# Edge preparation merged into the head attention, edge chunks fetched inside the counting stage

## What is computed

```python
def reference(x, src, dst, ...):
    # layer 1: attention among the 8 heads of each node, then a sum over edges
    Q, K, V = (x @ Wq), (x @ Wk), (x @ Wv)                 # each as [N, 8 heads, 32]
    score = softmax(einsum('nhd,ngd->nhg', Q, K) / sqrt(32), axis=-1)
    x1 = einsum('nhg,ngd->nhd', score, V).reshape(N, 256)
    attn_out = segment_sum(x1[dst] * x1[src], dst, N)      # = x1 * (adjacency counts @ x1)
    ...                                                    # O, norm, FFN, norm, GRU, norm
    # layer 2: h = x @ W, weights exp(-leaky_relu(s[src] + t[dst])), a normalised sum over edges
    return layernorm(x + relu(weighted_sum / row_sum))
```

## Time and profile before

| | |
|---|---|
| median of 3 runs | 2529.97 us (2529.07 to 2530.01) |
| profiled execution: its own time | 2528.87 us |
| profiled execution: its span in the trace | 2527.2 us |
| PE busy | 2398.2 us (95% of the span) |
| DVE busy | 1908.9 us (76%) |
| ACT busy | 1309.4 us (52%) |
| POOL busy | 575.0 us (23%) |
| granted TensorE clock, mean | 0.982 |
| preparation | until the first load of the attention at 62.02 us |
| head attention | until the counting's first instruction at 374.48 us |
| counting | until about 1092 us |
| update, then weighing | the rest |

### The profile page before, as it was taken

How to read it: one execution, slowest core, us unless ns; L and a number is a source line. 1 busy time by engine, 2 the same in 40 slices (tenths; PEclk the granted TensorE clock), 3 DMA queues, 4 the chain that set the end, 5 groups by cost and what they waited for, 6 DMA issues and landing times.

```text
span 2527.2 us, 47159 instructions
## 1 busy us (share of the span) xinstructions
PE 2398.2 (95%) x16169; PEld 1994.7 (79%) x16169; DVE 1908.9 (76%) x3148; ACT 1309.4 (52%) x2239; POOL 575.0 (23%) x628
## 2 busy tenths in 40 slices
PE   3899979999999999979999999899999999999995
PEld 2577757877777777756666666699999999999995
DVE  5788866666666666637777776799989898989895
ACT  3233328888888888844444444555343334333432
POOL 4699970000000000024444443000101010101010
PEclk9999998999999999989999999899999999999998
DMA  2111102223223223260214210356464645464552
GB/s 81 54 46 46 46 25 109 110 119 128 110 115 133 110 110 137 110 207 30 68 65 128 74 44 30 90 127 122 93 124 92 123 90 123 97 114 90 121 104 54
DMA packets 406003, 240.04 MB, mean 95 GB/s; under 512 B 326288, under 2 KB 397584, under 8 KB 399568
## 3 DMA queue, kind: packets, MB, share of 16 engines
q1 hardware_dynamic: 397536, 228.12, 32.9%
q10 hardware_dynamic: 7056, 6.43, 0.7%
q0 software_dynamic: 1248, 3.41, 0.5%
HBM read 48.38 MB, written 110.84 MB: 63 GB/s over the span
## 4 chain that ended last, share of the span: by engine, by line
PE 47%; issue 33%; POOL 2%; SPq 1%; DMA 1%; ACT 1%; DVE 0%; POOLq 0%; ACTq 0%; DVEq 0%
PE b_pagg L1500 22%; PE u_hf L632 10%; PE u_mo L616 7%; PE b_pcounts L1511 6%; POOL d_rstd L1848 2%; PE u_tp L605 2%; PE u_tp L676 0%; DMA u_agg<-agg 0%; DMA agg<-b_sums 0%; ACT b_counts L1539 0%; ACT b_counts L1540 0%; SPq L557 0%; SPq L166 0%; SPq L564 0%; SPq L151 0%
## 5 line engine op out<-in xcount | busy, mean ns | idle before, releaser
L1870 PE MATMUL d_acc<-d_rows_high,d_weights_high 128*128 128x258 f32 x2401 | 679.4, 283 | 7.6 <-DVE d_weights_low L1742 5.4
L1871 PE MATMUL d_acc<-d_rows_low,d_weights_high 128*128 128x258 f32 x2401 | 678.2, 282 | 0.0
L1872 PE MATMUL d_acc<-d_rows_high,d_weights_low 128*128 128x258 f32 x2401 | 677.7, 282 | 0.0
L1500 PE MATMUL b_pagg<-x_parts,b_counts 128*128 128x512 f32 x2401 | 608.5, 402 | 0.0
L1819 ACT CAST d_weights_high<-d_weights 128x896 fp32r<-128x896 f32 x343 | 323.5, 944 | 485.7 <-PE d_acc L1872 292.7
L1500 PEld LDWEIGHTS b_pagg<-x_parts,b_counts 128*128 128x128 f32 x2401 | 437.6, 189 | 92.3
L1870 PEld LDWEIGHTS d_acc<-d_rows_high,d_weights_high 128*128 128x128 f32 x2401 | 454.7, 189 | 8.1 <-issue 8.1
L1871 PEld LDWEIGHTS d_acc<-d_rows_low,d_weights_high 128*128 128x128 f32 x2401 | 454.8, 189 | 0.3 <-issue 0.3
L1872 PEld LDWEIGHTS d_acc<-d_rows_high,d_weights_low 128*128 128x128 f32 x2401 | 454.7, 189 | 0.0
L1742 DVE TENSOR_TENSOR d_weights_low<-d_weights,d_weights_high 128x896 fp32r<-128x896 f32 x343 | 373.5, 1089 | 52.9 <-ACT d_weights_high L1819 51.3
L1176 DVE TENSOR_TENSOR b_lo_hot<-b_nodes,b_ends 128x1024 bf16<-128x1024 f16 x392 | 269.9, 688 | 179.6 <-PE b_pcounts L1511 179.2
(11 more groups left out here) (162 smaller groups left out, 2793.8 us busy)
## 6 DMA issues: line engine op xcount, KB each, us to landing
edge_counts<-b_counts SPq DMA_DIRECT2D x49, 1568.0 KB, 5.2
node_table<-u_table SPq DMA_DIRECT2D x7, 903.0 KB, 4.9
qx<-in_x SPq DMA_DIRECT2D x49, 128.0 KB, 2.0
x_table<-x_tile ACTq DMA_DIRECT2D x49, 128.0 KB, 1.7
agg<-b_sums SPq DMA_DIRECT2D x49, 128.0 KB, 4.2
u_x<-x_table SPq DMA_DIRECT2D x7, 896.0 KB, 5.3
u_agg<-agg SPq DMA_DIRECT2D x7, 896.0 KB, 7.4
u_nodes<-in_x SPq DMA_DIRECT2D x7, 896.0 KB, 5.1
```

Of the source, the lines that this page charges most:

```text
L1500: last = nc.tensor.matmul(pagg[:, o, :], ca[:, o, hi, :], x1_parts[:, hi].rearrange("p m d -> p (m d)"), start=(hi == 0), stop=(hi == TILE ...
L1870: nc.tensor.matmul(acc[:, r, 0:HT], a, high[:, t, :], start=(t == 0), stop=False)
L1871: nc.tensor.matmul(acc[:, r, 0:HT], a, low[:, t, :], start=False, stop=False)
L1872: return nc.tensor.matmul(acc[:, r, 0:HT], b, high[:, t, :], start=False, stop=(t == TILES - 1))
```

## The change

One part merges the first two stages. `prepare_edges` is gone; its line search (`find_lines`) now consists of small functions that the attention's own engine programs call at certain steps, so one barrier and one clearing fall away. SP loads `e_dst` ahead of the first tile and the weights, and `e_dst_next` behind the fourth tile. DVE runs the one-hot comparisons ahead of its first step; PE runs the 202 counting matmuls ahead of its step 3; DVE makes the index in its step 1, between the products and their sums; POOL then issues one gather.

A second part moves the chunks. Only chunk 0 is fetched and split in the merged stage (behind DVE's last step), the other 25 in the counting stage: every second step POOL copies one column of the index and issues a gather, DVE splits the ends in six operations behind its batches 3 to 7, SP stores the result to HBM (`edges_found`) and loads it back with a transposing DMA into a buffer for two steps. PE's transposes, ACT's share of the splitting and the big `edge_ends` are gone. The test of the edges compares neighbouring line numbers now (two small matmuls) and stands behind the last step.

A third part swaps two places on ACT: the keys of tile T-1 are copied ahead of the exponential of T-2, not behind it.

The diff, cut to its core:

```diff
-def attention_rows(nc, kit, c, w, x, x1_out, parts):
+def attention_rows(nc, kit, c, w, x, x1_out, dst, pairs, found, chunk, early, parts_after):
...
             @block.sync
...
+                    if isinstance(T, int) and T == QUAD - 1:
+                        lines["load_next"](sp)
+
+                lines["load_dst"](sp)
                 tile_steps(sp, step, 0)
+                lines["first_ends"](sp)
...
             @block.tensor
             def _(pe):
                 def step(T, u):
+                    if isinstance(T, int) and T == 3:
+                        lines["count_lines"](pe)
+                        lines["next_lines"](pe)
...
                 tile_steps(pe, step, 6)
+                lines["sum_bad"](pe)
...
             @block.scalar
...
                         nc.scalar.copy(xT[:, u % 2, :], tpv[:, u % 2, 0:D]).then_inc(xT_ready, 1)
+                    t, q = T - 1, (u - 1) % QUAD
+                    if is_tile(t):
+                        act.wait_ge(qkv_in_psum, T)
+
+                        free(act, products, t, 2)
+                        nc.scalar.copy(keys[:, q % 2, :], pqk[:, q % 2, D:2 * D]).then_inc(k_ready, 1)
                     if is_tile(T - 2):
                         act.wait_ge(shifted, T - 1)
                         q = (u - 2) % QUAD
                         nc.scalar.activation(sc[:, q], sc[:, q], ACT.Exp, scale=SCORE_SCALE).then_inc(exped, 1)
                     t, q = T - 1, (u - 1) % QUAD
                     if is_tile(t):
-                        act.wait_ge(qkv_in_psum, T)
-
-                        free(act, products, t, 2)
-                        nc.scalar.copy(keys[:, q % 2, :], pqk[:, q % 2, D:2 * D]).then_inc(k_ready, 1)
                         free(act, av_ready, t, QUAD)
                         nc.scalar.copy(v[:, q, :], tpv[:, q % 2, D:2 * D]).then_inc(v_ready, 1)
...
             @block.gpsimd
...
+                    if isinstance(T, int) and T == 1:
+                        lines["first_gather"](pool)
...
             @block.vector
...
+                    if isinstance(T, int) and T == 1:
+                        lines["first_lines"](dve)
+                    if isinstance(T, int) and T == 2:
+                        lines["spans"](dve)
...
+                lines["search"](dve)
                 tile_steps(dve, step, 2)
+                lines["first_chunk"](dve)
+                lines["judge"](dve)
...
-def prepare_edges(nc, kit, memory, c, dst, pairs):
...
+    def store(self, sp, found, stored):
+        sp.dma_start(found, self.found[:].rearrange("p j e -> p (j e)")).then_inc(stored, 16)
+
+    def load(self, sp, found, loaded):
+        sp.dma_start_transpose(self.ends[:], found).then_inc(loaded, 16)
...
-def count_and_sum(nc, kit, c, x1_parts, dst, src, x1, agg, counts, over, prefetch):
+def count_and_sum(nc, kit, c, x1_parts, dst, src, x1, agg, counts, pairs, found, chunk, over, prefetch):
...
         def sync(sp):
...
+                    if next_chunk(s, k, build):
+
+                        t = chunk_of(s, i)
+                        hold(sp, split, SPLITS * t + SPLITS)
+                        chunk.store(sp, found, found_stored)
+                        hold(sp, found_stored, 16 * t + 16, 16)
+                        hold(sp, ends_ready, s + 2)
+                        chunk.load(sp, found, ends_loaded)
...
         def gpsimd(pool):
...
+                        if k == 0 and use:
+                            hold(pool, ends_loaded, 16 * chunk_of(s, i), 16)
                         if use:

-                            pool.wait_ge(hot, BATCHES * (s - 1))
+                            hold(pool, hot, BATCHES * (s - 1))
...
+                    if next_chunk(s, k, build):
+                        t = chunk_of(s, i)
+                        if use:
+
+                            hold(pool, split, SPLITS * t)
+                        nc.gpsimd.tensor_copy(chunk.idx_now[:], chunk.idx[:, bass.ds(t + 1, 1)]).then_inc(picked, 1)
+                        nc.gpsimd.tensor_copy(chunk.middle_now[:], chunk.middle[:, bass.ds(t + 1, 1)]).then_inc(picked, 1)
+                        hold(pool, picked, 2 * t + 2)
+                        chunk.gather(nc, pairs, chunk.idx_now[:, 0:1])
...
         def vector(dve):
...
                         compare(nc, key1[:, b % 2], keys[:], ends[:, k, 1, at, :], ALU.is_equal).then_inc(hot, 1)
+                        if next_chunk(s, k, build):
+                            next_ends(chunk_of(s, i), b)
```

More of the change, by code:

```diff
@@ L211, in ps @@
             return tmp.enter_context(nc.psum_tensor(name, shape, F32))
+        tpv, pqk = ps("q_tp_and_v", [P, 2, 512]), ps("p_qk", [P, 2, 512])
+        raw = ps("p_scores", [P, 2, 512])
+        x1_sum = ps("p_x1", [P, 2, 512])
+        lines = find_lines(nc, kit, Kit(nc, tmp, kit.whole), early, c, chunk, dst, pairs, found, x1_sum, raw, parts_after)
+        parts = lines["parts"]
         wqkv = sb("wqkv", [P, KC, 3 * D])
@@ L373, in step @@
                                                 ALU.add).then_inc(av_ready, 1)
+                lines["constants"](pool)
                 tile_steps(pool, step, 2)
@@ L1373, in count_and_sum @@
         walk = EdgeWalk(kit, tmp, nc, "l0", False, pagg[:, 0, :])
+        picked, split = kit.sem("b_chunk_picked"), kit.sem("b_chunk_split")
+        found_stored, ends_loaded = kit.sem("b_found_stored"), kit.sem("b_ends_loaded")
+        SPLITS = 6
         consts = kit.sem("b_consts")
@@ L1389, in steps, with next_chunk, chunk_of @@
             step(TILES, TILES % 2, (TILES - 1) // 2, False, True)
+        def next_chunk(s, k, build):
+            return build and k == 0 and not (isinstance(s, int) and s == TILES - 1)
+        def chunk_of(s, i):
+            return 0 if isinstance(s, int) and s == 0 else i + 1
         def older(s, k, i):
@@ L1465, in add_halves, with next_ends @@
                         .then_inc(sums_ready[o], 1)
+                def next_ends(t, b):
+                    if b == 3:
+                        dve.wait_ge(chunk.fetched, 16 * t + 32)
+                        dve.wait_ge(picked, 2 * t + 2)
+                        chunk.split_high(nc, split)
+                        chunk.place(nc, chunk.middle_now[:, 0:1], split)
+                    elif b == 4:
+                        dve.wait_ge(split, SPLITS * t + 2)
+                        if not isinstance(t, int) or t >= 1:
+                            dve.wait_ge(found_stored, 16 * t)
+                        chunk.split_low(nc, split)
+                    elif b == 5:
+                        chunk.square_place(nc, split)
+                    elif b == 6:
+                        dve.wait_ge(split, SPLITS * t + 4)
+                        chunk.key(nc, split)
+                    elif b == 7:
+                        dve.wait_ge(split, SPLITS * t + 5)
+                        chunk.own_keys(nc, split)
                 def step(s, k, i, build, use):
@@ L1920, in build @@
     counts = nc.dram_tensor("edge_counts", [ROWS, ROWS], F16, kind="Internal").ap()
+    found = nc.dram_tensor("edges_found", [P, 2 * REACH], F16, kind="Internal").ap()
     with ExitStack() as ctx:
@@ L1925, in build, with parts_after @@
             memory = Kit(nc, held, kit)
-            with kit.stage() as k:
-                prepare_edges(nc, k, memory, c, a["dst"], a["pairs"])
-            parts = memory.sb("x1_parts", [P, TILES, 2, D], F32R)
-            with kit.stage() as k:
-                attention_rows(nc, k, c, w, a["x"], x1, parts)
+            memory.sb("first_weights_home", [P, UpdateWeights.FIRST_WORDS])
+            chunk = ChunkEnds(memory, kit)
+            with kit.stage() as k, ExitStack() as early:
+                early.enter_context(nc.sbuf_tensor("x1_parts_of_first_tiles", [P, 10, 2, D], F32))
+                kept_parts = []
+                def parts_after():
+                    early.close()
+                    kept_parts.append(memory.sb("x1_parts", [P, TILES, 2, D], F32R))
+                    return kept_parts[0]
+                attention_rows(nc, k, c, w, a["x"], x1, a["dst"], a["pairs"], found, chunk, early, parts_after)
+            parts = kept_parts[0]
             with kit.stage() as k:
@@ L1934, in build @@
                 prefetch = {}
-                counting = count_and_sum(nc, k, c, parts, a["dst"], a["src"], x1, agg, counts, over, prefetch)
+                counting = count_and_sum(nc, k, c, parts, a["dst"], a["src"], x1, agg, counts, a["pairs"], found, chunk, over, prefetch)
                 held.close()
```

307 lines of the change are left out of this document (157 added, 150 removed).

## The result

The changed kernel takes 2470.55 us (median of 4 executions, 2467.38 to 2472.09) where the kernel before takes 2529.99 (4 executions, 2529.07 to 2530.68): a ratio of 0.9761, with a 95% interval of 0.9747 to 0.9775. The forecast was 2474, with a range of 2466 to 2488. The profiled execution of after took 2471.91 us (span 2470.2), that of before 2528.9, so the two traces differ by 57.0 us.

What follows compares the result with a forecast made beforehand. PE was taken to bound the counting, a ring of DVE and ACT the attention's step, and waits the preparation. 2528.9-50.9-6.5+1.6+0.5 = 2473.6, with 1.1 back about 2474 us; range 2466 to 2488.

Steps and rivals of the forecast that it cites:

- The head: Start of the merged stage up to tile 1's products: new order of loads, counts and index saves 50.9 us.
- the two bounds of the loads: First loads in the head: there at 7.4 us if they share nothing, 11.4 if they wait for one another; 9.5 taken.
- Keys first: Attention loop: copying keys ahead of the exponential makes PE the bound at 5.60 us a step, saving 6.5 us.
- PE's loads for nobody: Sign in the attention loop: PE's weight loads, which waited 0.34 us for POOL before, would wait for no engine.
- The end: End of the merged stage: 20 more semaphores to clear, charged 1.6 us, at most 2.2.
- Chunk 0 and the test at no charge: End of the merged stage: DVE's six operations (about 2 us), store, load and test are covered; uncovered, some 10 us.
- Rival B: End of the merged stage: DVE's operations with two SBUF inputs hold up POOL, 2.6 us more, 2476.6; chance 0.1.
- The counting: Counting stage: DVE's six added operations every second step are hidden, 0; only the first step charged, 0.5 us.
- the charge for the first gather: Counting's first step: its gather is issued in the step that wants it; 0.5 us, between 0 and 3.
- Chain of a chunk: Counting: store, transposing load and POOL's copies take about 7 us, within a step of 14.6 us.
- Rivals C: Counting: DVE's additions delay a pair's second comparison, costing PE half their time, 18 us, so 2492; chance 0.1.
- D: Counting: a chunk's chain outlasts a 14.6 us step, the excess paid 24 times; at 17.5 us, 2543; chance 0.03.

Runs made afterwards that it cites:

- e3: The changed kernel with PE's 202 counting matmuls one step earlier, ahead of the matmuls of tile 1's products: 2466.54 us.
- e1: The changed kernel with ACT's old order, the exponential of the tile two steps back ahead of the keys' copy: 2479.20 us.
- e2: The kernel before with only ACT's swap, the keys' copy ahead of the exponential: 2520.01 us, ratio 0.9966.
- e6: The changed kernel with the preparation's 20 semaphores held for the whole program, so not cleared at the merged stage's end: 2467.21 us.
- e5: The changed kernel with DVE's six operations on chunk 0 at the end of its step 6 instead of behind its last step: 2476.14 us.
- e11: The changed kernel with each chunk's transposing load held back until batch 4 of 8 of the step after: 2469.91 us.
- e8: The changed kernel with each chunk's transposing load held back until ACT has kept batch 7 of 8 of the step after: 2582.64 us.
- e12: The changed kernel run again without any edit, giving its second trace: 2471.45 us.
- e4: The changed kernel with 18 more unused transposes on PE in each of the merged stage's last three steps: 2464.80 us.

## Why the prediction was right, step by step

- **The head**: 50.9 us forecast, 51.6 measured, and each mark on the way within half a us: loads 9.5 (9.66), tile 1's products on PE 19.1 (19.3), counts 24.8 (24.63), index 25.3 (sums behind it at 24.94), next products 28.1 (27.66). That the middle between the two bounds of the loads came out is partly luck: no row chose it, and in the twelve traces of the merged stage PE first uses tile 1 between 9.45 and 10.96 us. The added wait on DVE came as named, 5 us forecast and 5.09 measured. What I didn't ask is whether it had to be there: in e3 it is gone, and the products start 4.9 us earlier.
- **Keys first**: 6.5 us forecast, 7.9 measured (8.0 and 8.7 in e1 and e2). The mechanism was right in the main: DVE waits 0.4 us for the keys and PE is the bound. But the sign "PE's loads for nobody" didn't come: they waited for POOL in 21 of 38 steps, so POOL's 5.46 lay closer to the bound than the working had it. Of the 1.4 us between forecast and measurement, 0.8 are the mean step, 5.58 instead of 5.60, and 0.6 what I had taken off for the ends of loops. That the mean step came so close is partly luck. In the step shown PE needs 4.65 us from line 320 to line 311 and 0.86 for line 311, together 5.51, where the working had 4.75 and 0.83: twelve matmuls that began behind a wait for POOL took 339.46-336.95 = 2.51 us in the step of before that I read, 2.41 in after's (280.98-278.57), so 0.1 us of the wait was inside what I had taken for PE's own time. In the other direction, the step of 5.84 at each turn of the loop wasn't in the working at all.
- **The end**: 1.6 forecast, 2.8 in the first trace, 1.3 in the second (315.3-289.0 against 25.0). The clearing is 1.0 of it (e6: 1.0 to 1.3), and I had put it too high by taking the barriers' time as clears; 1.5 of the first trace is PE's lower clock, which comes and goes.
- **Chunk 0 and the test at no charge**: right, as the cover held; DVE ends its own work at 310.3, 1.0 us ahead of the last store's issue, and then waits 1.83 us for PE to give the verdict at 312.3. But the six operations took 10 us (295.8 to 306.1) instead of the 2 in my working, so the cover, from DVE's last step to the store at 311.3, was nearly used up.
- **Rival B**: the mechanism is there, with the sides reversed. I priced DVE holding POOL (2.6 us); in the trace DVE's operation is the later one and waits, 3.37 and 3.83 us, and POOL pays 0.07 (1.33 instead of 1.26). By the Trainium skill, "SBUF — State Buffer", section "Who interferes with whom", whichever of the two issues first holds the shared ports for its whole instruction; the trace agrees, and e5 shows what it costs without cover: 4.4 us.
- **The counting**: 0.5 us forecast, -0.4 measured; in the first step DVE's `e_high` starts at 323.38 without a wait, so the charge for the first gather wasn't paid. Chain of a chunk: about 7 us forecast, 4.5 to the landing and 0.5 for the copies measured. Rivals C and D are refuted for this kernel. D's threshold of 14.6 us for the chain agrees with e11, where the chain, from DVE's last operation to POOL's copies, is 14.6 us long and costs nothing. In e8 it is 20.4 us long, for which D's sum gives 24*(20.4-14.6) = 139 us and the trace 129. That is close partly by luck: PE waits for 81 us only, and D had no term for the 49 us by which the matmuls became slower.

## What to carry to other kernels

Follow the order of the changed program on each engine, mark by mark, with durations from the old trace; here this gave a head right to 1 us, and the marks also name the next edit: an added wait whose cause can stand one step earlier in another queue. Before work is put beside POOL's long operations, ask who issues second: here a 0.3 us operation lasted as long as what POOL was doing, which was free under cover and cost 4 to 6 us without it. For a chain that feeds a later step, delay it on purpose by two amounts: the free one and the one that is paid bound the slack and give the price, of which a part can be a lower clock after the wait and not the wait itself.

## What the runs showed of the hardware that I had not expected

- PE's granted clock fell between groups of matmuls with pauses of about 2.5 us: at the end of the merged stage the mean was 0.66 from 295 to 300 us, after a wait of 2.53 us, and twelve matmuls took 4.54 us instead of 2.86. It isn't the same each time: groups behind an equal wait also took 2.86 (e12, 2.54 us), and of the traces that don't alter this end some have one slow group, some two. In e8's counting, where PE waited some 3.4 us for each chunk, the mean was 0.93.
- An operation of DVE with a single input in SBUF, `e_high` (128x128 int32 from int32), was held as long by POOL's running operation (3.37 us) as those with two inputs; sums along an axis and reciprocals in the same steps (0.19 to 0.22 us) were not.
- Adding 70 matmuls to PE's program in early stages went with 1.7 to 1.8 us more at each turn of a loop some 1600 us later; adding 54 (e4) did not.
- Twenty more semaphores to clear between two barriers went with 1.0 to 1.3 us, 0.05 to 0.06 each. A transposing load of 64 KB lands after 2.3 us (median of 25).
